# Layer 3's input normalised after its transpose, by two products on TensorE, with the projection's halves last in each step

## What is computed

```python
h = jnp.maximum(_layernorm(x, axis=-1), 0.0)      # over the 64 features
x = x + _L2_gnn_ref(h, adj, L2_gnn_weight, L2_gnn_query, L2_gnn_key_p)
h = jnp.maximum(_layernorm(x, axis=-1), 0.0)
x = x + _L3_gnn_ref(h, adj, L3_gnn_W, L3_gnn_a)
```

## Time and profile before

| | us |
|---|---|
| median of 3 runs | 1460.42 (1458.31 to 1466.05) |
| the profiled execution, its own time | 1465.91 |
| its span, first to last instruction | 1464.2 |
| busy in the span: DVE / POOL / PE / ACT | 1195.2 / 960.1 / 956.3 / 855.2 |

### The profile page before, as it was taken

The page is one execution under the profiler, slowest core; times in us unless marked ns, Lnnn a source line. Parts: engine busy times, 40 slices in busy tenths (PEclk is TensorE's granted clock), DMA queues, the critical chain, the costliest instruction groups (busy, mean ns, idle before and its releaser), DMA issues. The chain is left out here.

```text
span 1464.2 us, 16972 instructions
## 1 busy us (share of the span) xinstructions
PE 956.3 (65%) x4663; PEld 672.8 (46%) x4663; DVE 1195.2 (82%) x1552; ACT 855.2 (58%) x2899; POOL 960.1 (66%) x983
## 2 busy tenths in 40 slices
PE   3665447542898886498899966566616755756591
PEld 1433113212687775387788832222205655652240
DVE  5994689985999999999999159999976998947571
ACT  5864336664575465356787726777983548654330
POOL 4214776626887866398787468887666787647770
PEclk9887777866899998799999987877856777887796
DMA  9838987514222431012111054533226564438875
GB/s 286 272 102 299 323 243 239 167 58 141 60 83 84 117 92 37 29 35 75 51 51 37 30 166 134 146 115 110 84 97 189 156 185 115 132 119 248 240 236 139
DMA packets 108294, 202.19 MB, mean 138 GB/s; under 512 B 48320, under 2 KB 56800, under 8 KB 106144
## 3 DMA queue, kind: packets, MB, share of 16 engines
q0 software_dynamic: 38384, 128.36, 28.6%
q1 hardware_dynamic: 68840, 72.46, 15.6%
q10 hardware_dynamic: 968, 0.21, 0.1%
HBM read 149.97 MB, written 55.21 MB: 140 GB/s over the span
## 5 line engine op out<-in xcount | busy, mean ns | idle before, releaser
L1092 ACT ACTIVATE big<-big 128x64 f32<-128x64 f32 x1496 | 370.8, 339 | 172.1 <-DVE big L1869 161.0
L806 POOL TENSOR_TENSOR big<-big 128x512 f32<-128x512 f32 x373 | 376.5, 1040 | 123.0 <-DVE big L1869 108.1
L1912 DVE TENSOR_REDUCE big<-big 128x32 f32<-128x2048 f32 (+4 forms) x126 | 297.7, 2362 | 4.3
L1447 PE MATMUL PS<-big,ident 128*128 128x512 f32 x348 | 188.8, 704 | 117.2 <-ACT big L1092 70.5
L1466 PE MATMUL PS<-ident,big 128*128 128x128 f32 x1740 | 232.5, 294 | 42.2 <-POOL big L806 35.1
L1466 PEld LDWEIGHTS PS<-ident,big 128*128 128x128 f32 x1740 | 218.4, 154 | 52.1 <-issue 24.8
L1904 DVE TENSOR_TENSOR big<-big,PS 128x2048 f32<-128x2048 f32 (+4 forms) x84 | 198.5, 2363 | 17.3 <-PE PS L1478 14.5
L1447 PEld LDWEIGHTS PS<-big,ident 128*128 128x128 f32 x348 | 76.3, 226 | 228.0 <-issue 203.8
L779 POOL DMA_INDIRECT big<-tab,SI x142 | 138.0, 972 | 48.6 <-issue 45.0
L779 POOL DMA_INDIRECT big<-h_rows,SI x142 | 137.9, 971 | 38.4 <-issue 29.3
L1463 PE MATMUL PS<-big,ident 128*128 128x512 f32 x174 | 105.9, 769 | 55.3 <-POOL big L806 51.8
(11 more groups left out here) (182 smaller groups left out, 1682.3 us busy)
## 6 DMA issues: line engine op xcount, KB each, us to landing
big<-in_adj SPq DMA_DIRECT2D x16, 1024.0 KB, 6.4
own<-big SPq DMA_DIRECT2D x48, 256.0 KB, 2.0
big<-own SPq DMA_DIRECT2D x48, 256.0 KB, 3.4
big<-xs SPq DMA_DIRECT2D x8, 1024.0 KB, 8.7
tab<-big SPq DMA_DIRECT2D x32, 132.0 KB, 2.8
own<-big SPq DMA_DIRECT2D x32, 132.0 KB, 1.9
big<-own SPq DMA_DIRECT2D x16, 264.0 KB, 4.0
big<-in_x SPq DMA_DIRECT2D x16, 256.0 KB, 6.8
```

What stands on the lines that cost most here:

```text
L806: ins = pool.tensor_tensor(bd(wbuf[:, i % NWB, j, :]), bd(rows[:, k + j, :]), over_d(S[:, h, k + j, :], B), ALU.mult)
L1092: ins = act.activation(to, row, ACT.Copy, scale=S[:, h, k + j, b:b + 1])
L1447: mm = pe.matmul(to.rearrange("p (b d) -> p b d", b=B), ident[:, :], rows[:, k, :].rearrange("p (b c) -> p b c", b=B)[:, :, 0:D], start=(k ...
L1912: run(dve.tensor_reduce(scores(u, t)[:, h, k:k + n, :].rearrange("p k b -> p (k b)"), bd(prod[:, 0:n * E]), AX.X, ALU.add))
```

## The change

The diff touches only u = 3 and what it shares. Layer 3's normalisation is no longer made on rows, but on the turned tile. TensorE turns the residual sum itself; a 128x128 matrix `centring` takes the mean off each group of 64 features, ScalarE squares the result, `averaging` puts the variance into every element of the group, ScalarE takes Ln and Exp over 512 columns, and one VectorE operation makes the normalised turned tile. The row mean, the variance's reduction and `end_norm` on VectorE, and `centre` on GpSimd, are gone for this layer.

```diff
@@ names of tiles and banks
-        def turn_bank(k):
-            return bank(2 if k < NT else 2 + k % 2)
+        turn_bank = bank(2)
+        x3T, sq3T, r3T, h3T = work[:, 6:8, :], sqn, hring, work[:, 4:6, :]
+        def c3_bank(t):
+            return bank(3 + 4 * (t % 2))
@@ SyncE and GpSimd
-                                store_halves(3, m - 6)
+                                store_halves(3, m - 7)
-                                centre(3, m - 3)
-                                put_rows(4, m - 6)
+                                put_rows(4, m - 7)
@@ ScalarE, step m (behind the copy of tile m-2's sum)
-                    norm(3, m - 3)
-                    s = m - 5
-                        if s >= 2:
-                            act.wait_ge(half_projected, 2 * (NT + s - 1))
-                        take_turned(hT3[:, s % 2, :])
-                    halves(3, m - 6, (0, 1))
+                    s = m - 3
+                        take_turned(x3T[:, s % 2, :])
+                    s = m - 4
+                        act.wait_ge(xc_made, NT + s + 1)
+                        act.activation(sq3T[:, s % 2, :], c3_bank(s), ACT.Square).then_inc(xc_squared, 1)
+                    s = m - 5
+                        act.wait_ge(xvar_made, NT + s + 1)
+                        act.activation(r3T[:, s % 4, :], bank(1), ACT.Ln, bias=epsc[:, 0:1]).then_inc(xvar_logged, 1)
+                        act.wait_ge(xvar_logged, NT + s + 1)
+                        act.activation(r3T[:, s % 4, :], r3T[:, s % 4, :], ACT.Exp, scale=-0.5).then_inc(xvar_rooted, 1)
                     if 0 <= m + 2 < NT:
                         take_turned(hTo[:, m % 2, :])
+                    halves(3, m - 7, (0, 1))
                     exp(3, m)
@@ TensorE, a turn and a half
-                    pe.wait_ge(turn_freed, k if k <= NT else k - 1)
+                    pe.wait_ge(turn_freed, k)
-                b = bank(4 + q) if l == 0 else bank(7 - 6 * q)
-                if t >= 1:
+                b = bank(4 + q) if l == 0 else bank(1)
+                if l == 3:
+                    pe.wait_ge(half_staged, m)
+                elif t >= 1:
                     pe.wait_ge(half_staged, m - 1)
@@ TensorE, step m (behind the queries)
-                        pe.wait_ge(h_made, 2 * NT + m - 5 + 1)
-                        turn_in_ring(norm_rows(3, m - 5))
-                            half(3, m - 6, q, hT3[:, (m - 6) % 2, :])
+                    t = m - 3
+                        turn_in_ring(X[:, t, :])
+                    t = m - 5
+                        if t >= 3:
+                            pe.wait_ge(half_staged, 2 * (NT + t - 2))
+                        pe.matmul(bank(1), averaging[:, :], sq3T[:, t % 2, :], start=True, stop=True).then_inc(xvar_made, 1)
+                    t = m - 4
+                        if t >= 2:
+                            pe.wait_ge(h0_made, NT + t - 1)
+                        pe.matmul(c3_bank(t), centring[:, :], x3T[:, t % 2, :], start=True, stop=True).then_inc(xc_made, 1)
...
                         add_up(3, m - 1)
+                    t = m - 7
+                        pe.wait_ge(xvar_logged, NT + min(t + 2, NT - 1) + 1)
+                        pe.wait_ge(h0_made, NT + t + 1)
+                        for q in range(2):
+                            half(3, t, q, h3T[:, t % 2, :])
@@ VectorE, step m (behind the scores of tile m)
-                            variance(3, m - 3)
-                            end_norm(3, m - 4)
                             t = m - 2
                                 tell(dve.tensor_tensor(X[:, t, :], bank(6), X[:, t, :], ALU.add), sum_used, NT + t + 1)
-                            row_mean(3, t)
+                            t = m - 5
+                                dve.wait_ge(xvar_rooted, NT + t + 1)
+                                if t >= 2:
+                                    dve.wait_ge(half_projected, 2 * (NT + t - 1))
+                                tell(dve.scalar_tensor_tensor(h3T[:, t % 2, :], c3_bank(t), 0.0, r3T[:, t % 4, :],
+                                                              ALU.max, ALU.mult), h0_made, NT + t + 1)
```

More of the change, by code:

```diff
@@ L102 @@
 for m in range(-2, NT + 10):
-    for what, t in (("next", m - 5), ("own", m + 2)):
+    for what, t in (("next", m - 3), ("own", m + 2)):
         if 0 <= t < NT:
@@ L989, in take_turned @@
                 act.wait_ge(turned, k + 1)
-                act.activation(to, turn_bank(k), ACT.Copy).then_inc(turn_freed, 1)
+                act.activation(to, turn_bank, ACT.Copy).then_inc(turn_freed, 1)
             def halves(l, t, parts):
@@ L1200, in near @@
                         act.activation(aT[:, t % 2, :], bank(0), ACT.Copy).then_inc(aggT_made, 1)
-                    norm(3, m - 3)
+                    s = m - 3
+                    if 0 <= s < NT:
+                        if s >= 2:
+                            act.wait_ge(xc_made, NT + s - 1)
+                        take_turned(x3T[:, s % 2, :])
+                    s = m - 4
+                    if 0 <= s < NT:
+                        act.wait_ge(xc_made, NT + s + 1)
+                        if s >= 2:
+                            act.wait_ge(xvar_made, NT + s - 1)
+                        if s < 2:
+                            act.wait_ge(var_made, 2 * NT)
+                        act.activation(sq3T[:, s % 2, :], c3_bank(s), ACT.Square).then_inc(xc_squared, 1)
                     s = m - 5
                     if 0 <= s < NT:
-                        if s >= 2:
-                            act.wait_ge(half_projected, 2 * (NT + s - 1))
-                        take_turned(hT3[:, s % 2, :])
-                    halves(3, m - 6, (0, 1))
+                        act.wait_ge(xvar_made, NT + s + 1)
+                        if s >= 4:
+                            act.wait_ge(h0_made, NT + s - 3)
+                        else:
+                            ring_free(act, 3 * NT + s)
+                        act.activation(r3T[:, s % 4, :], bank(1), ACT.Ln, bias=epsc[:, 0:1]).then_inc(xvar_logged, 1)
+                        act.wait_ge(xvar_logged, NT + s + 1)
+                        act.activation(r3T[:, s % 4, :], r3T[:, s % 4, :], ACT.Exp, scale=-0.5).then_inc(xvar_rooted, 1)
                     if 0 <= m + 2 < NT:
@@ L1377, in turn_in_ring @@
                 if k >= 1:
-                    pe.wait_ge(turn_freed, k if k <= NT else k - 1)
-                return turn(turn_bank(k), rows).then_inc(turned, 1)
+                    pe.wait_ge(turn_freed, k)
+                return turn(turn_bank, rows).then_inc(turned, 1)
             def half(l, t, q, hT_):
                 m = 2 * (NT * (l // 3) + t) + q
-                b = bank(4 + q) if l == 0 else bank(7 - 6 * q)
-                if t >= 1:
+                b = bank(4 + q) if l == 0 else bank(1)
+                if l == 3:
+                    pe.wait_ge(half_staged, m)
+                elif t >= 1:
                     pe.wait_ge(half_staged, m - 1)
@@ L1552, in near @@
                         mm.then_inc(q_made, 1)
-                    if 0 <= m - 5 < NT:
-                        pe.wait_ge(h_made, 2 * NT + m - 5 + 1)
-                        turn_in_ring(norm_rows(3, m - 5))
-                    if 0 <= m - 6 < NT:
-                        pe.wait_ge(turn_freed, TURN_OF["next", m - 6] + 1)
-                        for q in range(2):
-                            half(3, m - 6, q, hT3[:, (m - 6) % 2, :])
+                    t = m - 3
+                    if 0 <= t < NT:
+                        pe.wait_ge(sum_used, NT + t + 1)
+                        turn_in_ring(X[:, t, :])
+                    t = m - 5
+                    if 0 <= t < NT:
+                        pe.wait_ge(xc_squared, NT + t + 1)
+                        if t >= 3:
+                            pe.wait_ge(half_staged, 2 * (NT + t - 2))
+                        pe.matmul(bank(1), averaging[:, :], sq3T[:, t % 2, :], start=True, stop=True).then_inc(xvar_made, 1)
+                    t = m - 4
+                    if 0 <= t < NT:
+                        pe.wait_ge(turn_freed, TURN_OF["next", t] + 1)
+                        if t >= 2:
+                            pe.wait_ge(h0_made, NT + t - 1)
+                        pe.matmul(c3_bank(t), centring[:, :], x3T[:, t % 2, :], start=True, stop=True).then_inc(xc_made, 1)
                     t = m + 2
```

1 line of the change is left out of this document (removed).

## The result

| | before | changed |
|---|---|---|
| median, us (range, runs) | 1462.7 (1458.31 to 1466.05, 4) | **1496.56** (1495.81 to 1504.01, 4) |
| profiled execution / its span, us | 1465.91 / 1464.2 | 1495.88 / 1494.1 |
| DVE / POOL / PE / ACT busy, us | 1195.2 / 960.1 / 956.3 / 855.2 | 1151.9 / 942.6 / 969.4 / 869.7 |

The changed kernel is slower: ratio 1.0259, 95% interval 1.0229 to 1.0289. VectorE works 43 us less, 34 of them in unit 3, and the kernel takes 34 us more. The median of before has four runs here; the three that the prediction started from gave 1460.42.

The account below looks back on a forecast made before the run. Unit 3 was taken as bound by VectorE's own work. Terms +28.7, -3 and +11 give +36.7 on the profiled 1465.9, so 1502.6; that execution lay 5.5 above the median, hence 1497 us, range 1478 to 1512.

Parts of the forecast that it names:

- Term 1: Unit 3, steps 9 to 15: a loop through TensorE's adding up makes them 113.3 us instead of 84.6, +28.7.
- Term 2: Unit 3, steps 2 to 8: VectorE saves 11.4 us, most lost to waits; net -3 us, between -7 and +1.
- Term 3: From tile 15's weighing to the last table write: 32 us instead of 21.0, +11, between +7 and +14.
- The ring: Unit 3, steps 7 to 15: weighing, copies, turn, projection, adding up, halves, exp, divide, next weighing; 18.6 us in step 10.
- all slow: Upper bound for steps 9 to 15, with TensorE slow throughout: +36 us instead of +28.7.
- the time of 1487: Whole-kernel forecast if transposes took 81 ns each: 15.6 us for the 192 of steps 9 to 15 instead of 26.
- Two waits: Unit 3: own rows' turn waits for ScalarE's copy of layer 3's turned tile; halves, then exp, wait behind the adding up.
- What the removal was worth: VectorE in unit 3: 1.64 us a tile, 26 us over 16 tiles; 23 us in steps 2 to 15.
- A: Unit 3: VectorE is the only bound and the halves come early enough; 1437 us with the old tail; chance 0.06.
- B: Unit 3: TensorE stays ahead and ScalarE's own work is the loop; steps 9 to 15 take 77, kernel 1456; chance 0.06.
- C: Unit 3: longer idle keeps TensorE at 1.2 GHz, 0.22 us a transpose; +57, about 1517 us; chance 0.06.

Follow-up runs that it names:

- reordered_tail: `reordered` with the halves projected one step earlier (tile m-6) and those of tiles 10 to 15 in two banks instead of one: 1444.1 us, ratio 0.989.
- halves_before_sum: The changed kernel with the halves of tile m-7 ahead of the adding up on TensorE alone: 1473.0 us, ratio 1.007 against the kernel before.
- own_first: The changed kernel with own rows turned and copied ahead of layer 3's tile, halves and exp still last: 1502.1 us, ratio 1.027 against the kernel before.
- reordered: The changed kernel with own rows first, halves ahead of the adding up, exp ahead of the half copies, VectorE's operation in a four-buffer ring: 1460.1 us, ratio 0.998.
- before_halves_last: The kernel before with its halves moved behind the adding up and directly ahead of exp, normalisation left on rows: 1498.0 us, ratio 1.026.
- no_norm: The kernel before with layer 3's normalisation left out altogether, nothing in its place: 1427.8 us, ratio 0.975.
- bhl_centre_late: `before_halves_last` with GpSimd's centring of tile m-3 moved behind its weighing of tile m-1: 1486.8 us, ratio 1.018 against the kernel before.

## Why the prediction was right

The forecast was 1497 and the time is 1496.56. The mechanism is the one forecast; that the number is met to half a microsecond is luck, as the differences below show. By the prediction's own terms, for one profiled execution each:

| | predicted | measured |
|---|---|---|
| Term 1, steps 9 to 15 | +28.7 | +30.8 |
| Term 2, steps 2 to 8 | -3 | -4.8 |
| Term 3, the tail | +11 | +12.7 |
| sum | +36.7 | +38.8 |

The spans of the two profiled executions differ by 29.9 only, since the one of before came to unit 3 7.6 us later (last section) and took 1.3 us more behind it. The prediction had counted nothing outside unit 3. The medians differ by 34: 2.8 less than forecast, from a median before that is 2.3 higher than the one it was added to.

**The ring was right, and its terms can be read in step 10.** From the weighing to the turn 8.85 (7.75 + 1.1 predicted), to the projection 0.87 (0.65), to the adding up 1.71 (1.45), to the first half 5.18 (4.2), to the next weighing 3.45 (3.5). Sum 20.06, predicted 18.6. What was sized too low is TensorE after its idle time: turn and projection ran at half the rate (1.08 and 1.91 us; 0.60 and 1.16 in `reordered_tail`), where I had taken a value between the two, and the adding up took 0.167 a transpose in this step for my 0.13. Step 9 went the other way: 24.55 for 26.1, because its 52 transposes took 5.98 us, 0.115 each, where I had carried over 7.91. In all the 192 transposes of steps 9 to 15 took 28.2 us for my 26, and Term 1 is too low by as much. The bound "all slow" counted 0.152 for a transpose, not the 0.22 of half the clock; the mean came out at 0.147.

**The tail.** From step 17 to step 20 a step took 5.7 us for my 4.8, and the halves of the last two tiles 2.45 each for 2.1. The rest took less than I had it, and Term 3 is 1.7 us too low.

**Rate of the transposes.** The prediction took 0.114 us as the fastest rate. No run has a stream of them much faster: 5.98 us for 52 here, 3.66 for 32 in `reordered_tail`, and 5.84 for 52 in `halves_before_sum`, 0.112 each, the fastest in any trace. The 81 ns of the Trainium skill (TensorE: Matmul & The Clock Gate, Back-to-back issue gap) did not appear, nor the time of 1487 that it gave.

**Two waits, one shown.** The prediction gave both waits as the cause. `halves_before_sum` shows the second, the halves behind the adding up: 27.0 of the 30.8 us. For the first, the own rows' turn behind layer 3's copy, no run shows a cost: `own_first` gained nothing, with another turn in its place, and `reordered` goes from 88.4 to 79.6 us with three orders changed at once. And the cost of the place is not a cost of the new normalisation: `before_halves_last` has it without.

**What the removal was worth** was set too low: 23 to 26 us, where VectorE's busy time in unit 3 fell by 34.3 and `no_norm` gained 37. The three groups that the changed kernel's unit 3 lacks account for 11.0 + 11.0 + 2.8 = 24.8 us; 9.3 more are in two short operations that were held beside GpSimd's centring, once beside its weighing too (3.56 us in step 7). Of before, in unit 3 (line, operation, times | busy us, mean ns | idle before):

```profile
L1869 DVE TENSOR_TENSOR big<-big,mx 128x40 f32<-128x40 f32 (+7 forms) x16 | 9.3, 580 | 0.5
L1839 DVE SCALAR_TENSOR_TENSOR big<-big 128x40 f32<-128x40 f32 (+7 forms) x16 | 6.6, 415 | 0.6
```

The same lines of the changed kernel:

```profile
L1906 DVE TENSOR_TENSOR big<-big,mx 128x40 f32<-128x40 f32 (+7 forms) x16 | 3.3, 203 | 0.6
L1876 DVE SCALAR_TENSOR_TENSOR big<-big 128x40 f32<-128x40 f32 (+7 forms) x16 | 3.3, 203 | 0.6
```

It didn't matter for the time, since VectorE was no longer the bound in steps 9 to 15. In steps 2 to 8 `halves_before_sum` parts Term 2: with the halves early they took 77.7 for 89.4, a gain of 11.7 (11.4 in the prediction), and the halves' place takes 6.9 of it back (8.4).

**The rivals.** A (VectorE alone decides) and B (ScalarE's own work decides) would have needed the halves early, which they are not in this kernel. `reordered` shows that B is near the truth for another order of the steps: 79.6 us in steps 9 to 15 for its 77, with ScalarE busy 69.4 of them. C (half the clock throughout) is out: 0.82 in steps 9 to 15, and 1.00 in the tail.

## What to carry to other kernels

Where engines run written-out steps in order, ask of each moved instruction whether it joins the ring that runs once a step. Here two projected halves and their two copies, 2 us of work a step, were put behind an adding up of 2 to 6 us. In the kernel before, that place alone cost 22 us with no instruction added. With the halves ahead of the adding up, the other ties cut and the tail shortened, the new normalisation gave a gain of 1%. Test the place and the work apart: the change as a whole hid a gain and a larger loss.

## What the runs showed that I had not expected

**A short VectorE operation can be held beside GpSimd for microseconds.** L1869, with two inputs in SBUF (the on-chip memory the engines share), took 0.18 to 0.27 us by itself and 0.60 to 1.75 beside a GpSimd centring of 1.04 us, and then ended within 0.1 us of the centring's end; moving only the centring took this away (`bhl_centre_late`). The Trainium skill (SBUF — State Buffer, Who interferes with whom) states that such an instruction contends with a GpSimd instruction that reads SBUF. The trace agrees with that. The same section of the Trainium skill states that the order of issue decides which of the two blocks the other. The starts in the profile don't show this: in `before_halves_last` VectorE's is 0.53 us ahead (1249.17 against 1249.70), and yet VectorE is the one held; the profile's times on GpSimd are rough.

The hold can also last over several GpSimd instructions. Unit 2, same instruction stream in both kernels; of before, VectorE:

```profile
994.97 7.62 DVE L2016 TENSOR_TENSOR nshift<-ln 128x8 f32<-128x8 f32 x1 [0.24 <-ACT ln L1173]
```

and GpSimd beside it:

```profile
995.30 5.03 POOL L806 TENSOR_TENSOR big<-big 128x512 f32<-128x512 f32 x5
1000.30 1.26 POOL L815 TENSOR_TENSOR big<-big,rows 128x512 f32<-128x512 f32 x1
1001.53 1.03 POOL L790 TENSOR_TENSOR big<-big,stats 128x512 f32<-128x512 f32 x1
```

Eight columns took 7.62 us, to the end of GpSimd's seventh operation. In the changed kernel the same operation started 0.53 us ahead of GpSimd's five (at 994.59) instead of 0.33, and was not held:

```profile
994.06 0.17 DVE L2053 TENSOR_TENSOR nshift<-ln 128x8 f32<-128x8 f32 x1
```

The difference between executions ahead of unit 3 goes with this one operation. It took 7.6 to 7.7 us in eight of the thirteen profiled executions, whose tile 1 is weighed from 1116.0 to 1117.5, and was not held in the other five, where that weighing starts from 1109.9 to 1112.6. `before_halves_last` and the changed kernel reach it at 993.87 and 994.06, and tile 1 at 1116.29 and 1109.88. A second long hold, 6.88 us at 904.17 in the execution of before alone, left no such mark: it starts unit 3 with the other seven. That execution took 1465.91, 3.2 us above its median. Whether such holds account for the spread of `halves_before_sum`, 17 us, isn't settled: only one of its ten executions has a trace.
